# Normalising X of images 1 to 7 in channel order by broadcast rows of scale and shift

## What is computed

```python
x = x + attention(_ln_c(x))          # eps 1e-6, over the 512 channels of each pixel
t = _to_tokens(x)                    # 8 x 1024 x 512
t = t + _L0_ffn_ref(_ln_t(t), ...)   # one-hot nibbles -> 3-layer nets of width 160, twice
x = _from_tokens(t, x)
# attention: q, k, v = xs @ W.T + b (8 heads of 64); softmax(q k^T / 8) v; @ Wo.T + bo
```

## Time and profile before

| | |
|---|---|
| runs | 2573.31 us median of 3 (2571.03 to 2573.49) |
| the profiled execution: its own time | 2568.86 us |
| its span, first to last instruction | 2567.1 us |
| mean granted PE clock | 0.992 of full |
| PE / DVE / ACT / POOL busy | 2459.3 / 1945.7 / 1731.8 / 918.3 us |
| first T of the edges at | 276.94, 589.70, 902.57, 1216.60, 1530.11, 1843.83, 2159.13 us |

### The profile page before, as it was taken

How to read it: one execution, slowest core, us unless ns; L and a number is a source line. 1 busy time by engine, 2 the same in 40 slices (tenths; PEclk the granted TensorE clock), 3 DMA queues, 4 the chain that set the end, 5 groups by cost and what they waited for, 6 DMA issues and landing times.

```text
span 2567.1 us, 37185 instructions
## 1 busy us (share of the span) xinstructions
PE 2459.3 (96%) x13216; PEld 2015.1 (78%) x13216; DVE 1945.7 (76%) x3605; ACT 1731.8 (67%) x3083; POOL 918.3 (36%) x814
## 2 busy tenths in 40 slices
PE   7999999999999999999999999999999999999986
PEld 6788878887788777887878877788777887778874
DVE  5777777787777877778777787777867778677766
ACT  4777557774677746777377773777747776477754
POOL 2344414443144432443414433244422444234431
PEclk9999999999999999999999999999999999999998
DMA  7233213241223312324122340232402324023220
GB/s 276 62 83 116 86 31 93 75 132 66 66 67 79 123 63 66 78 66 136 50 77 68 79 141 33 78 87 60 155 17 84 81 70 144 30 86 79 59 77 33
DMA packets 80550, 215.14 MB, mean 84 GB/s; under 512 B 10384, under 2 KB 10608, under 8 KB 74608
## 3 DMA queue, kind: packets, MB, share of 16 engines
q1 hardware_dynamic: 80368, 212.77, 27.7%
HBM read 102.63 MB, written 25.17 MB: 50 GB/s over the span
## 4 chain that ended last, share of the span: by engine, by line
PE 77%; DVE 12%; ACT 7%; issue 2%; POOL 1%; DMA 1%; SPq 0%; ACTq 0%; DVEq 0%
PE pT L473 15%; PE pJ L439 10%; PE pO L488 9%; PE pO L489 9%; PE pS L460 7%; PE pS L461 7%; PE po L626 6%; PE pv L599 3%; ACT PR L706 2%; PE pv L439 2%; DVE PL L890 2%; ACT PH L740 2%; POOL PR L391 1%; PE pa L637 1%; DVE nmax L858 1%
## 5 line engine op out<-in xcount | busy, mean ns | idle before, releaser
L391 POOL TENSOR_SCALAR PR<-PR,rinv 128x1024 f32<-128x1024 f32 x512 | 577.6, 1128 | 1219.4 <-DVE rinv L862 1219.4
L740 ACT ACTIVATE PH<-pT 128x512 fp32r<-128x512 f32 x1024 | 558.7, 599 | 360.4 <-PE pT L473 347.1
L890 DVE TENSOR_TENSOR PL<-pT,PH 128x512 fp32r<-128x512 f32 x1024 | 657.6, 684 | 180.1 <-ACT PH L740 178.0
L858 DVE TENSOR_REDUCE nmax<-pS 128x1 f32<-128x1024 f32 x512 | 623.6, 1218 | 146.2 <-PE pS L461 145.3
L706 ACT ACTIVATE PR<-pS,nmax 128x1024 f32<-128x1024 f32 x512 | 576.3, 1126 | 4.2 <-DVE nmax L858 1.0
L473 PEld LDWEIGHTS pT<-ident,PR 128*128 128x128 f32 x4096 | 466.3, 141 | 128.9 <-POOL PR L391 47.8
L473 PE MATMUL pT<-ident,PR 128*128 128x128 f32 x4096 | 545.7, 275 | 21.7 <-DVE PL L890 15.4
L488 PE MATMUL pO<-PH,VS 128*128 128x512 f32 x1024 | 417.9, 408 | 6.4 <-DVE PL L890 6.4
L460 PE MATMUL pS<-KHL,QS 128*128 128x512 f32 x1024 | 411.4, 402 | 2.9 <-ACT PR L706 1.6
L489 PE MATMUL pO<-PL,VS 128*128 128x512 f32 x1024 | 404.0, 395 | 0.0
L461 PE MATMUL pS<-KHL,QS 128*128 128x512 f32 x1024 | 402.9, 393 | 0.0
(11 more groups left out here) (171 smaller groups left out, 3060.0 us busy)
## 6 DMA issues: line engine op xcount, KB each, us to landing
KHL<-HL SPq DMA_DIRECT2D x192, 256.0 KB, 3.4
X<-in_x SPq DMA_DIRECT2D x64, 512.0 KB, 6.5
WQ<-wqk_split SPq DMA_DIRECT2D x62, 512.0 KB, 4.3
QS<-HL SPq DMA_DIRECT2D x192, 128.0 KB, 3.0
WO<-wo_split SPq DMA_DIRECT2D x16, 1024.0 KB, 6.6
out<-X SPq DMA_DIRECT2D x16, 1024.0 KB, 4.7
KHL<-wv_split SPq DMA_DIRECT2D x14, 1024.0 KB, 8.5
KHL<-KHL SPq DMA_DIRECT2D x16, 512.0 KB, 4.3
```

The lines of the kernel that those rows point to most:

```text
L391: pool.tensor_scalar(PR[g % 2][:, :], PR[g % 2][:, :], M["rinv"][:, g:g + 1], 1.0, ALU.mult, ALU.mult)\
L740: act.activation(PH[ck % 2][:, 4 * half:4 * half + 4, (g % 4) * P:(g % 4 + 1) * P], pT[half][:, :].rearrange("p (k n) -> p k n", k=4), ACT ...
L858: dve.tensor_reduce(nmax[:, g:g + 1], pS[g % 2][:, :], AX.X, ALU.max, negate=True).then_inc(S["a_max"], 1)
L890: dve.tensor_tensor(PL[ck % 2][:, ks, qs], pT[half][:, :].rearrange("p (k n) -> p k n", k=4), f32(PH[ck % 2][:, ks, qs]), ALU.subtract).th ...
```

## The change

For images 1 to 7 X stays in channel order. PE still transposes it to tokens, but DVE takes the statistics straight from PSUM (pt), and XT isn't written. Scale and shift, 128x16 numbers, are transposed (PE, new step M), copied (ACT), written to DRAM as 16 rows of 128, and read back so that every partition holds both rows in full (RROW, 128x2048, 1 MB). DVE multiplies X by the scale row (M, 8 instructions of 128x512, reading X with a stride of 8 elements), POOL adds the shift row (8 instructions), both in SBUF. ACT and DVE then split XP into XH and XL as before, now from SBUF. The 32 transposes B of an edge and POOL's scaling are gone. The first-layer features stand once (NF = 32 rows instead of 96), so its three matmuls use the same 32 rows of the array; DVE writes a third of the elements of F and clears F itself; START has four small loads fewer. All three tables are new.

```diff
@@ sync_program
         if i + 1 < N_IMG:
-            wait("f_back", i + 1, 4)
+            wait("f_rc", i, 1)
+            sp.dma_start(dram["rn"], M["RNT"][:, :]).then_inc(S["f_row"], 16)
+            wait("f_row", i, 16)
+            rows = dram["rn"].rearrange("(a s) p -> a (s p)", a=2).unsqueeze(0).to_broadcast([P, 2, HW])
+            sp.dma_start(M["RROW"][:, :, :], rows).then_inc(S["f_rows"], 16)
@@ gpsimd_program
+        elif kind == "M":
+            for t in range(CT):
+                wait("f_mul", img - 1, 4 * g + t + 1)
+                xs = M["XP"][:, t, g * 512:(g + 1) * 512]
+                pool.tensor_tensor(xs, xs, M["RROW"][:, 1, g * 512:(g + 1) * 512], ALU.add).then_inc(S["f_xn"], 1)
@@ tensor_program
-                pe.matmul(ph[m][:, :], W0[rows, :], FT[rows, q * 512:(q + 1) * 512], start=True, stop=True)\
+                pe.matmul(ph[m][:, :], W0[:, m, :], FT[:, q * 512:(q + 1) * 512], start=True, stop=True)\
...
-                wait("f_copy", i, n - 2)
+                wait("f_copy" if i == 0 else "f_stat", i, n - 2)
...
-        elif kind == "B":
+        elif kind == "M" and n == 0:
+            wait("f_var", i, 7)
+            pe.transpose(pt[2][0:2 * ST, 0:P], M["f_rn"][:, :, :].rearrange("p a s -> p (a s)"), ident[:, :]).then_inc(S["f_rt"], 1)
+        elif kind == "B" and i == 0:
@@ scalar_program
+        elif kind == "M" and n == 0:
+            wait("f_rt", i - 1, 1)
+            act.activation(M["RNT"][:, :], pt[2][0:2 * ST, 0:P], ACT.Copy).then_inc(S["f_rc"], 1)
...
+                wait("f_xn", i - 1, 4 * (n // 4 + 1))
+                source = M["XP"][:, :, cs]
+            act.activation(XH[:, :, cs], source, ACT.Copy).then_inc(S["f_hi"], 1)
@@ vector_program
+        elif kind == "M":
+            wait("f_rows", i - 1, 16)
+            for t in range(CT):
+                tokens = M["X"][:, t, :].rearrange("p (m e) -> p e m", e=2 * CT)[:, n::2, :]
+                cs = slice(n * 512, (n + 1) * 512)
+                dve.tensor_tensor(M["XP"][:, t, cs].rearrange("p (e m) -> p e m", e=CT), tokens,
+                                  M["RROW"][:, 0, cs].rearrange("p (e m) -> p e m", e=CT), ALU.mult).then_inc(S["f_mul"], 1)
```

More of the change, by code:

```diff
@@ L118, in build @@
                 M[p + "_" + n] = sb(p + "_" + n, [P, ST])
+        rn = sb("f_rn", [P, 2, ST])
+        M["f_rn"], M["f_r"], M["f_nb"] = rn, rn[:, 0, :], rn[:, 1, :]
+        M["RNT"] = sb("RNT", [2 * ST, P])
         M["r1"] = sb("r1", [P, ST])
@@ L172, in build @@
             "small": [(b_qk[:, :], bqk), (b_v[D:P, :], bv), (bo_all[:, :], bo_rep), (ramp[:, :], ramp_d),
-                      (iota[:, :], iota_d), (M["w1r"][:, :], w1),
+                      (iota[:, :], iota_d), (M["w0r"][:, :], w0), (M["w0m"][:, :], w0mask), (M["w1r"][:, :], w1),
                       (w2r[:, 0, :], w2[:, 0, :]), (w2r[0:D, 1, :], w2[0:D, 1, :]), (w2r[D:P, 1, :], w2[0:D, 1, :])],
         }
-        for m in range(3):
-            rows = slice(m * NF, (m + 1) * NF)
-            setup["small"] += [(M["w0r"][rows, :], w0[:, m * P:(m + 1) * P]), (M["w0m"][rows, :], w0mask)]
         B = {}
@@ L216 @@
 EDGE = {
[L217 to L226, removed]
+    "tensor": """T0 T1 T2 E65 E66 E67 T3 T4 T5 T6 T7 O0 O1 O2 O3 M0 O4 O5 O6 O7 U0 U1 U2 U3 U4 U5 U6 V0 U7 V1 V2 V3 V4 V5
+        V6 F0 V7 L0 F1 F2 Q0 F3 L1 L10 Q1 L2 L20 L11 L3 L12 L21 Q2 L22 L13 P0 L23 P1 Y0 Q3 A0 R0 R1 R2 R3 A1 R4
+        R5 A2 R6 R7 A3""",
@@ L232 @@
         R1 R2 L23 R3 R4 R5 R6 R7""",
[L233 to L235 removed]
+    "vector": """E67 H0 H1 H2 H3 O0 O1 O2 O3 O4 O5 O6 U0 U1 U2 U3 S10 O7 S15 S11 U4 S12 U5 U6 U7 S13 S20 S25 S21 L0 S22
+        S23 L10 L1 L11 L2 L3 L12 S14 L13 S24""",
+    "gpsimd": """H0 F0 F2""",
 }
@@ L404, in gpsimd_program @@
                     pool.tensor_tensor(xs, xs, M["bo_all"][:, :], ALU.add).then_inc(S["b_bias"], 1)
[L405 to L408, removed]
+        elif kind == "M":
[3 more added lines that the diff above has]
+                pool.tensor_tensor(xs, xs, M["RROW"][:, 1, g * 512:(g + 1) * 512], ALU.add).then_inc(S["f_xn"], 1)
+        elif kind == "N" and img == 0:
             wait("f_half" if g == 10 else "f_var", img, 7)
@@ L783, in scalar_program @@
         elif kind == "B":
[L784 to L788, removed]
+            cs = slice(n * P, (n + 1) * P)
+            if i == 0:
+                wait("f_back", i, n + 1)
+                source = pt[n % 3][:, :].rearrange("p (t n) -> p t n", t=CT)
+            else:
+                if n == 0:
+                    wait("b_y", i - 1, 8)
+                wait("f_xn", i - 1, 4 * (n // 4 + 1))
+                source = M["XP"][:, :, cs]
+            act.activation(XH[:, :, cs], source, ACT.Copy).then_inc(S["f_hi"], 1)
         elif kind == "V":
@@ L1081, in vector_program @@
         elif kind == "T":
-            wait("f_copy", i, n + 1)
-            dve.bn_stats(M["f_stats"][:, n, :], XT[n][:, :]).then_inc(S["f_stat"], 1)
+            if i == 0:
+                wait("f_copy", i, n + 1)
+                dve.bn_stats(M["f_stats"][:, n, :], XT[n][:, :]).then_inc(S["f_stat"], 1)
+            else:
+                wait("f_tok", i, n + 1)
+                dve.bn_stats(M["f_stats"][:, n, :], pt[n % 3][:, :]).then_inc(S["f_stat"], 1)
+        elif kind == "M":
[5 more added lines that the diff above has]
+                                  M["RROW"][:, 0, cs].rearrange("p (e m) -> p e m", e=CT), ALU.mult).then_inc(S["f_mul"], 1)
         elif kind == "N":
@@ L1089, in vector_program @@
             cs = slice(n * P, (n + 1) * P)
-            dve.tensor_tensor(XL[:, :, cs], pt[n % 3][:, :].rearrange("p (t n) -> p t n", t=CT), f32(XH[:, :, cs]),
-                              ALU.subtract).then_inc(S["f_lo"], 1)
+            source = pt[n % 3][:, :].rearrange("p (t n) -> p t n", t=CT) if i == 0 else M["XP"][:, :, cs]
+            if i > 0:
+                wait("f_mul", i - 1, 8)
+            dve.tensor_tensor(XL[:, :, cs], source, f32(XH[:, :, cs]), ALU.subtract).then_inc(S["f_lo"], 1)
         elif kind == "V":
```

71 lines of the change are left out of this document (38 added, 33 removed).

## The result

The changed kernel takes **2643.75 us** (median of 4 runs, 2641.21 to 2645.96), the kernel before beside it 2572.17 us (4 runs): a ratio of 1.0282, 95% interval 1.0266 to 1.0298. It is slower, by 71.6 us or 10.2 for each of the seven edges. The profiled execution took 2643.31 us, with a span of 2641.5 and a mean granted clock of 0.984.

The account below looks back on a forecast made before the run. PE was taken as the bound, with DVE the second limit of an edge. 9.0 us an edge times seven plus 0.7 in LAST gave +64: 2633 profiled, 2637 us as median; own range 2610 to 2660, with rivals 2580 to 2672.

Parts of the forecast that it names:

- O0 later by 0.8: Start of the O stage: O0 starts at 286.9, 0.8 us later than before, behind OL0 on DVE.
- Scales ready before O3 ends: DVE's scales before step M: ready before O3 ends at 298.2, with two us less ahead of f_nb's 299.3.
- Rows on every partition at 305.8: Scale and shift through DRAM: write 2.2 us, broadcast 4.7, rows landed at 305.8 (304.6 to 310.4).
- Rival C: Write and broadcast of the rows: broadcast 8.5 us, write 3.0, +4.6 an edge more, 2669 us; chance 0.12.
- M takes 12.4 us by turns: DVE's eight multiplications alternate with POOL's adds: 8 x 0.605 + 6 x 1.26 = 12.4 us.
- V0 at 321.35: V0 on PE: starts at 321.35, after XL0, which waits for POOL's last adds and ends at 321.3.
- V0 to the first layer, clock included: PE from V0 to V7's end at 346.05, F1 still to come; low clock +1.5 us an edge (0 to 2.5).
- First layer +0.7: First layer's three matmuls on the same array rows: +0.7 us an edge (0.3 to 1.04) and in LAST.
- Sum +64: Whole kernel: 6.8 + 0.7 + 1.5 = 9.0 us an edge, seven times 63, plus 0.7 in LAST: +64 us.
- Rival A: Step M: no turns between DVE and POOL, M takes 4.8 us, no cold clock, +11, 2584 us; chance 0.19.
- Rival B: Edges: PE's saving stays as rows come in time, V0 by about 313.9 to break even, 2556 us; chance 0.09.
- PE's saving of 2.6 an edge: PE's own work in an edge: 3.5 for transposes less 0.2 and 0.7 falls by 2.6 us.

Follow-up runs that it names:

- e10: The changed kernel with six of POOL's eight bias adds held back until after f_rn; 2637.43 us, ratio 1.0256.
- e1: The changed kernel without POOL's eight adds of the shift row in each edge; 2605.27 us, ratio 1.0134.
- e2: The changed kernel with X read without a step in the multiplication, POOL's adds kept; 2626.41 us, ratio 1.0219.
- e5: The kernel before with only the first-layer part of the change (features once, on 32 rows); 2578.53 us against 2570.06, ratio 1.0030.
- e3: The changed kernel with X read without a step and without POOL's adds of the shift row; 2588.32 us, ratio 1.0066.
- e9: e6 with six of POOL's eight bias adds held back until DVE's scale and shift are done; 2580.81 us, ratio 1.0039.
- e6: The changed kernel reordered: statistics and scales sooner, multiplications placed one by one between additions, POOL's last four adds after all eight; 2621.69 us, ratio 1.0195.
- e4: The changed kernel with the multiplication's inputs exchanged, RROW first and strided X second; 2640.95 us, ratio 1.0279.

## Why the prediction came out as it did

The forecast was 2637, the measured time 2643.75. The mechanism is the one it named: multiplications and adds in turns set V0. Its sum is 64 us where the profiled executions differ by 74.5, 9.0 an edge instead of 10.6, and part of its closeness is luck, since two errors in M go against each other. Its terms stand so:

- **O0 later by 0.8**: 286.90, as worked out, and for its reason (1.95 us of waiting for OL). The first T of this execution comes 0.28 us sooner than before, so within the edge it is 1.1 later, in all seven.
- **Scales ready before O3 ends**: wrong. They were ready at 299.04, where two us less than the 299.3 of before would be 297.3, because two small operations took 1.22 us each beside POOL's bias adds. In the earlier trace rows f_nb took 0.17, after POOL had finished; the change moved the chain forward into POOL's twelve microseconds. I had counted the instructions ahead of it and not the engine beside it. It holds up the residual add behind it, and PE waits 0.54 us before O4. The 0.46 before O2 have another reason: the pair of OL takes 4.58 us beside POOL, before 3.44. With both, O5's add, which M stands behind, ends 1.5 us later than the walk's 304.9. e10 takes both away and gains 6 us. It gains no more, for PE's first twelve matmuls behind the wait for OL take 4.2 to 4.4 us in four of its seven edges and 2.9 in the others, as in all seven of the changed kernel, and in one edge M waits 1.4 us for the rows.
- **Rows on every partition at 305.8**: issued at 301.10, landed in 4.4 us, 305.5. That is 5.8 us behind f_rn's copy (299.41 to 299.68), where the prediction's sign was 7. The write took 1.4 instead of 2.2, which made up for most of the late scales. Rival C's slow rows did not come. DVE was not waiting for them: O5's add ended at 306.49.
- **M takes 12.4 us by turns**: 14.0 (306.41 to 320.40). Two errors of opposite sign. The strided multiplication takes 1.10 from start to start alone (e1) and not 0.605, for which the prediction had no row; it stands there only in a sentence of rival C, so this much of C came true. And a pair in turns is shorter than its parts: 1.95 us where 1.10 + 1.26 would be 2.36. e2 shows the same without the step, 1.68 against 0.605 + 1.26 = 1.87, and its M takes 11.4 us: 1.0 less than the 12.4, and the step adds 2.6. The Trainium skill has a rule on the first ("SBUF — State Buffer", Door 1: The DMA port swizzle): consecutive accesses within 16 bytes of a partition keep full rate, so fp32 can be read with a step of up to 4 elements. The step here is 8. The measurement agrees, 1142 against 682 ns for one; no run here has a smaller step than 8 but 1.
- **V0 at 321.35**: 323.69, later by M's 1.6 and by DVE's start of it, 0.6. The gap before V0 put down to XL, one of the signs, did not come: XL0 ended at 323.3, and U4 to U6 at the low clock ended later.
- **V0 to the first layer, clock included**: from V0's start on 24.7 + 1.5 = 26.2 us; measured 25.9. This term held, and the late V0 makes the rest: the first layer starts 9.9 us later than before, where the walk gives 6.3 + 1.5 = 7.8 (its 6.8 counts F1, which comes behind the layer now). The clock fell as the earlier trace rows had it, to 0.55 in 321 to 327. V0's first four matmuls take 2.06 us instead of 1.17, and its first eight 1.25 us longer than before.
- **First layer +0.7**: +1.06 by e5's medians, at the bound of 1.04. The group takes 0.90 us, not 0.70, since the excess of 0.2 at its two ends stays. Four groups would be 1.84 us an image; part of that is hidden (e5).
- **Sum +64**: 74.5 between the profiled executions, 71.6 between the medians. PE's busy time, forecast as hardly lower, is 10.6 higher.
- **Rival A** (no turns) is what e1 and e3 make of the kernel: 2605 with the step, 2588 without. Its 2584 comes near only without the step, and without the adds at all. **Rival B** needed V0 at 313.9. e9 reaches that and still is 0.4% slower, about 10 us; the first layer's price by e5 is 8.5.
- **PE's saving of 2.6 an edge** is nowhere to be seen, because the transposes stood in front of V0, and V0's start is now set by DVE and POOL. In e9, where V0 is in time, PE spends it on the waits for VS.

## What to carry to other kernels

Elementwise work on SBUF on DVE and on POOL at once shared one place in these runs: write it down as one queue before deciding that it's hidden, and look at the short operations behind a long one too, where a chain of six went from 1.2 us to 5.9 and one added wait on POOL gave 41 us back (e6 to e9). An elementwise operation that gathers with a step in its free dimension has to be priced by its own row, here 1.14 us instead of 0.68. When two times are subtracted, both have to hold the same ends: the 0.44 of the row groups had 0.2 us of switching in it, and the 3 x 0.2345 had not. Where work is taken from the busiest engine, first ask which engine it goes to and whether that engine is the one waited for at the end of the stage.

## What the runs showed of the chip

- A 128x512 fp32 tensor_tensor of DVE with two SBUF inputs takes 0.68 us, with one of them at a step of 32 bytes 1.14.
- A DVE and a POOL tensor_tensor of that size, both on SBUF, repeat in turns at 1.95 us with the step and 1.68 without, less than the sum of the two alone (2.36 and 1.87, from start to start). With the strided tensor as second input (e4) a pair takes 2.07, and in six of seven edges DVE kept its place for four instructions while POOL's add lasted 4.35 us.
- DVE operations on 128x8 in SBUF take up to 1.2 us instead of 0.17 while POOL adds 128x512 tiles: four in a row in e6, two in the changed kernel.
- Three matmuls of 32 rows and 512 columns take 0.90 us to the next instruction in the same rows of the array, and 0.44 on different rows. Both hold 0.2 us over matmuls of 0.2345.
- A broadcast of 8 KB of DRAM to 128 partitions, 1 MB, lands in 4.4 us, like a store of that size.
